# First attention of a two-layer audio tower: exponentials of two duos in one ScalarE instruction, its tail interleaved with the feed-forward start, GpSimd's blanks split up behind its chains of norms

## The reference, cut to what matters

```python
h = _L0_tok_ref(x, w, b)                        # keep 179 of 256 tokens, by score
h = h + _L0_attn_ref(_layernorm(h), ...)        # "first attention", additive:
    # score[h,t,s] = sum_d tanh(q[t,d] + k[s,d]) * ws[d] + bs;  softmax over s;  @ v;  @ Wo.T + bo
h = h + _L0_ffn_ref(_layernorm(h), ...)         # 192 -> 768, gelu, rounded to int8 steps, -> 192
h = h + _L1_attn_ref(_layernorm(h), ...)        # x rounded to int8 steps of max|x|/127 over ALL of x;
    # 12 heads of 16, base-2 softmax with a linear mantissa
h = h + _L1_ffn_ref(_layernorm(h), ...)         # 16 experts, each token through the one of largest gate
```

## Time and profile before

| | us |
|---|---|
| median of 3 runs (lowest, highest) | 1291.1 (1290.3, 1291.1) |
| profiled execution, its own time | 1291.22 |
| its span, first to last instruction | 1289.5 |
| first attention, first to last tanh | 64.5 to 803.2 |
| tail and feed-forward | 803.2 to about 905 |
| busy time: PE, DVE, ACT, POOL | 1088.6, 1071.3, 1006.7, 858.3 |

### The profile page before, as it was taken

The page is one execution under the profiler, slowest core; times in us unless marked ns, Lnnn a source line. Parts: engine busy times, 40 slices in busy tenths (PEclk is TensorE's granted clock), DMA queues, the critical chain, the costliest instruction groups (busy, mean ns, idle before and its releaser), DMA issues. The chain is left out here.

```text
span 1289.5 us, 44108 instructions
## 1 busy us (share of the span) xinstructions
PE 1088.6 (84%) x18872; PEld 823.3 (64%) x18875; DVE 1071.3 (83%) x2070; ACT 1006.7 (78%) x966; POOL 858.3 (67%) x931
## 2 busy tenths in 40 slices
PE   4866887888888788888779877899999999998796
PEld 3544665566566566566656655799566777776595
DVE  8988999999999999999999997577666777888342
ACT  3499999999999999999999999588445555544242
POOL 3099899898889889888888999775001233334354
PEclk9999999999999999999999999999999999999898
DMA  5799999930000000000000000110000200002451
GB/s 161 238 359 359 357 341 326 336 119 11 11 2 11 10 10 4 11 11 2 11 11 2 12 10 2 52 23 1 2 3 3 68 18 18 17 20 60 135 154 45
DMA packets 78547, 107.84 MB, mean 84 GB/s; under 512 B 6963, under 2 KB 76489, under 8 KB 78356
## 3 DMA queue, kind: packets, MB, share of 16 engines
q1 hardware_dynamic: 67894, 91.62, 21.8%
q0 software_dynamic: 5360, 8.02, 1.9%
q10 hardware_dynamic: 5104, 5.43, 1.5%
HBM read 18.32 MB, written 83.85 MB: 79 GB/s over the span
## 5 line engine op out<-in xcount | busy, mean ns | idle before, releaser
L1007 ACT ACTIVATE work<-work 128x2864 f32<-128x2864 f32 (+1 forms) x272 | 694.1, 2626 | 4.0 <-POOL work L446 3.0
L446 POOL TENSOR_TENSOR work<-shared 128x1253 f32<-128x1253 f32 (+1 forms) x272 | 612.9, 2268 | 87.7 <-PE psum L2050 77.7
L2050 PE MATMUL psum<-work,ws_place 128*32 128x179 f32 x8640 | 400.5, 323 | 139.4 <-ACT work L1007 131.1
L446 DVE TENSOR_TENSOR work<-psum,shared 128x1611 f32<-128x1611 f32 (+3 forms) x288 | 488.0, 1722 | 0.7 <-PE psum L2050 0.3
L2050 PEld LDWEIGHTS psum<-work,ws_place 128*32 128x32 f32 x8640 | 266.2, 111 | 239.7 <-ACT work L1007 181.0
L2250 PE MATMUL psum<-shared 32*32 32x179 f32 (+1 forms) x3456 | 99.1, 326 | 1.2 <-DVE peaks L1658 0.7
L1388 DVE SCALAR_TENSOR_TENSOR p_sb<-psum,bs_col,s_top 128x358 f32<-128x358 f32 x144 | 82.0, 570 | 14.9
L996 ACT ACTIVATE pt_region<-psum,bs_neg 128x384 f32<-128x384 f32 x144 | 89.0, 619 | 3.6 <-PE psum L2062 3.6
L902 POOL DMA_INDIRECT xs_dram<-w_store,slot_i x24 | 28.5, 1188 | 81.3 <-DVE slot_i L1758 75.2
L1385 DVE TENSOR_REDUCE s_top<-psum 128x2 f32<-128x358 f32 x144 | 71.7, 498 | 9.5 <-PE psum L2050 8.7
L2062 PE MATMUL psum<-ident,p_sb 128*128 128x128 f32 x416 | 78.6, 297 | 0.0
(11 more groups left out here) (444 smaller groups left out, 2010.6 us busy)
## 6 DMA issues: line engine op xcount, KB each, us to landing
xs_dram<-pad_row SPq DMA_DIRECT2D x23, 3088.0 KB, 28.5
pt_region<-xs_dram SPq DMA_DIRECT2D x19, 193.0 KB, 2.5
pt_region<-xs_dram ACTq DMA_DIRECT2D x19, 193.0 KB, 2.6
xs_dram<-pad_row SPq DMA_DIRECT2D x1, 2895.0 KB, 28.4
pt_region<-v_sb SPq DMA_DIRECT2D x22, 96.0 KB
work<-in_x SPq DMA_DIRECT2D x2, 768.0 KB, 9.8
work<-in_x ACTq DMA_DIRECT2D x2, 768.0 KB, 12.5
work<-in_L_ffn_W2T SPq DMA_DIRECT2D x1, 1536.0 KB
```

The source lines that it names most:

```text
L446: ins = eng.tensor_tensor(dst[:, a * KEEP:e * KEEP].rearrange("p (u s) -> p u s", s=KEEP), k[:, h * KP:h * KP + KEEP].unsqueeze(1).to_broa ...
L1007: act.activation(a, a, ACT.Tanh).then_inc(tanh_done, 1)
L2050: ins = pe.matmul(bank_s[p % 2][32 * quad:32 * quad + 32, at:at + KEEP], ws_place[:, j, :], arg_slot(n)[:, u * KEEP:(u + 1) * KEEP], start ...
```

## The change

Five edits:

1. `exps(b, n)` takes two duos (2n, 2n+1) in one ACT instruction of 768 columns, read out of both banks and written to both duos' places; the ninth duo stays alone. They stand after the tanh of groups 8, 12 and 16, and of groups 3 and 4 of the next batch. `turn_duo` waits accordingly, and the ninth duo always lies in the second bank. An ACT instruction of batch 15 that stood ahead of its last tanh (duo 4) now stands behind it.
2. In the tail PE does `ffn_turn(-1)` behind g of 3 instead of 2; `ffn_turn(0)` ahead of `ffn_hidden(0)` behind g of 5; `ffn_hidden(1)` behind g of 9; and `ffn_turn(1)` behind g of 11. Steps 0 and 1 of the feed-forward loop keep only `ffn_out`, and step 1 waits for the last residual add and its statistics.
3. ACT loads the gelu's table behind the first copy of a transposed input instead of ahead of it, and copies the second one ahead of batch 0's gelu.
4. DVE normalizes batch 2 at g of 2 of the tail and clips batch 0's hidden layer at g of 14, both out of the loop's first steps.
5. POOL's blanks behind the first one are cut into seven pieces, `later_blanks(j)`, and each stands behind `again_norms(j)`. The ones of v1 (`qv_blank` 3 and 4) are in the last piece, behind `again_norms(6)`. PE's wait for `qv_blank` 4 stays where it is.

```diff
+EXPS = -(-DUOS // 2)
...
+        pt_banks = psum[:, 2048:3072].rearrange("p (k c) -> p k c", c=512)
...
+        def pt_bank(k):
+            return bank_pt[1 if k == DUOS - 1 else k % 2]
         def duo(k):
...
             pool.memset(xn3[:, 1::2, :], 0.0).then_inc(qv_blank, 1)
-            pool.memset(ctx1[:, :, :], 0.0)
-            pool.wait_ge(wq_step, 6)
-            for n in (2, 3):
-                pool.memset(stage[n][:, 1, 0:D], 0.0)
-            pool.memset(ew2[:, 1, :], 0.0).then_inc(ew_blank, 1)
-            for n in range(2):
-                pool.memset(eh[n][:, :], 0.0)
-            for n in range(2):
-                pool.memset(q1[n][:, :, :], 0.0)
-                pool.memset(k1[n][:, :, :], 0.0)
-                ins = pool.memset(v1[n][:, :, :], 0.0)
-            ins.then_inc(qv_blank, 1)
-            pool.wait_ge(qv_blank, 2)
-            for n in range(2):
-                pool.memset(v1[n][:, :, HD:HD + 1], 1.0).then_inc(qv_blank, 1)
-                pool.memset(eh[n][:, D:D + 1], 1.0).then_inc(eh_blank, 1)
+            def later_blanks(n):
+                if n == 0:
+                    pool.memset(ctx1[:, :, :], 0.0)
+                    pool.wait_ge(wq_step, 6)
+                    for m in (2, 3):
+                        pool.memset(stage[m][:, 1, 0:D], 0.0)
+                if n in (1, 2):
+                    half = ew2[:, 1, EXPERTS * D // 2 * (n - 1):EXPERTS * D // 2 * n]
+                    ins = pool.memset(half, 0.0)
+                    if n == 2:
+                        ins.then_inc(ew_blank, 1)
+                if n == 3:
+                    for m in range(2):
+                        pool.memset(eh[m][:, :], 0.0)
+                if n in (4, 5):
+                    m = n - 4
+                    pool.memset(q1[m][:, :, :], 0.0)
+                    pool.memset(k1[m][:, :, :], 0.0)
+                    ins = pool.memset(v1[m][:, :, :], 0.0)
+                    if m == 1:
+                        ins.then_inc(qv_blank, 1)
+                if n == 6:
+                    pool.wait_ge(qv_blank, 2)
+                    for m in range(2):
+                        pool.memset(v1[m][:, :, HD:HD + 1], 1.0).then_inc(qv_blank, 1)
+                        pool.memset(eh[m][:, D:D + 1], 1.0).then_inc(eh_blank, 1)
...
                 again_norms(j)
+                later_blanks(j)
...
-            def exps(b, k):
-                p, w = b * DUOS + k, duo(k)
-                if k == 0:
+            def exps(b, n):
+                lo, hi = 2 * n, min(2 * n + 2, DUOS)
+                w = duo(hi - 1)
+                if n == 0:
                     need(act, ctx_psum, 2 * b - 2)
-                act.wait_ge(turned, p + 1)
-                act.activation(pt[b % 2][:, 0:w + 1, k, :],
-                               bank_pt[p % 2][:, 0:128 * (w + 1)].rearrange("p (s c) -> p s c", c=128),
-                               ACT.Exp, bias=bs_neg[:, :], scale=1.0).then_inc(exp_done, 1)
+                act.wait_ge(turned, b * DUOS + hi)
+                if hi - lo == 2:
+                    turned_keys = pt_banks[:, :, 0:384].rearrange("p k (s c) -> p k s c", c=128)
+                    act.activation(pt[b % 2][:, :, lo:hi, :].rearrange("p s k c -> p k s c"), turned_keys,
+                                   ACT.Exp, bias=bs_neg[:, :], scale=1.0).then_inc(exp_done, 1)
+                else:
+                    act.activation(pt[b % 2][:, 0:w + 1, lo, :],
+                                   pt_bank(lo)[:, 0:128 * (w + 1)].rearrange("p (s c) -> p s c", c=128),
+                                   ACT.Exp, bias=bs_neg[:, :], scale=1.0).then_inc(exp_done, 1)
...
                         act.activation(a, a, ACT.Tanh).then_inc(tanh_done, 1)
-                    if g % 2 and g >= 7 and real(b):
-                        exps(b, (g - 7) // 2)
-                    if g in (0, 1, 3, 4) and real(b - 1):
-                        exps(b - 1, DUOS - 4 + (0, 1, 3, 4).index(g))
-            act.preload_act_table(ACT.Gelu)
+                    if g in (8, 12, 16) and real(b):
+                        exps(b, (g - 8) // 4)
+                    if g in (3, 4) and real(b - 1):
+                        exps(b - 1, EXPS - 2 + g - 3)
...
-                if isinstance(i, int) and i == 0:
-                    ffn_gelu(i, par)
-                    ffn_turned(i, par)
-                else:
-                    ffn_turned(i, par)
-                    ffn_gelu(i, par)
+                ffn_turned(i, par)
+                ffn_gelu(i, par)
             ffn_turned(-1, 1)
+            act.preload_act_table(ACT.Gelu)
             staged(act, ffn_step, (1, 0))
...
+            def hidden_round(b):
+                dve.wait_ge(gelu_done, b + 1)
+                need(dve, y_psum, b - 1)
+                dve.tensor_scalar(hq[b % 2][:, :, 0:KEEP], gelu[b % 2].bitcast(I32).rearrange("p (c t) -> p c t", c=HT),
+                                  -128.0, 127.0, ALU.max, ALU.min).then_inc(hq_ready, 1)
             for b in range(B + 1):
...
                         ins.then_inc(hq_blank, 1)
+                        dve.wait_ge(f_xT_psum, 1)
+                        ffn_norm(2, 0)
+                    if b == B and g == 14:
+                        dve.wait_ge(hq_blank, 1)
+                        hidden_round(0)
             def ffn_step(i):
-                if real(i + 2):
+                if real(i + 2) and i > 0:
                     dve.wait_ge(f_xT_psum, i + 1)
                     ffn_norm(i + 2, i % 2)
                 if real(i - 2):
                     ffn_add(i - 2)
-                if real(i - 1):
+                if real(i - 1) and i > 1:
                     hidden_round(i - 1)
...
                 dve.scalar_tensor_tensor(r, y_int, s_out[:, :], r, ALU.mult, ALU.add).then_inc(f_added, 1)
-            def hidden_round(b):
-                dve.wait_ge(gelu_done, b + 1)
-                need(dve, y_psum, b - 1)
-                dve.tensor_scalar(hq[b % 2][:, :, 0:KEEP], gelu[b % 2].bitcast(I32).rearrange("p (c t) -> p c t", c=HT),
-                                  -128.0, 127.0, ALU.max, ALU.min).then_inc(hq_ready, 1)
...
                 p = b * DUOS + k
-                bank, src = bank_pt[p % 2], p_sb[p % 2]
+                bank, src = pt_bank(k), p_sb[p % 2]
                 pe.wait_ge(smax_done, p + 1)
-                need(pe, exp_done, p - 1)
+                need(pe, exp_done, EXPS * b + (k // 2 if k else -1))
                 for s in range(duo(k) + 1):
...
                     if g == 5:
-                        pe.wait_ge(exp_done, DUOS * b)
+                        pe.wait_ge(exp_done, EXPS * b)
                         pe.wait_ge(v_ready, b)
...
                         if b == B:
-                            pe.wait_ge(f_xT_ready, 1)
+                            pe.wait_ge(f_xT_ready, 2)
                         for t, bank in enumerate((bank_out, bank_pre)):
...
-                if not isinstance(i, int) or i > 0:
+                if not isinstance(i, int) or i > 1:
                     ffn_turn(i, par)
                     ffn_hidden(i, par)
+                if isinstance(i, int) and i == 1:
+                    pe.wait_ge(resid_added, 2 * B)
                 ffn_out(i, par)
...
                     after_scores(b, g)
-                    if b == B and g == 2:
+                    if b == B and g == 3:
                         pe.wait_ge(smax_done, B * DUOS)
                         pe.wait_ge(wq_step, 6)
                         ffn_turn(-1, 1)
                     if b == B and g == 5:
+                        ffn_turn(0, 0)
                         ffn_hidden(0, 0)
+                    if b == B and g == 9:
+                        ffn_hidden(1, 1)
                     if b == B and g == 11:
-                        ffn_turn(0, 0)
+                        ffn_turn(1, 1)
             pe.wait_ge(hq_blank, 1)
-            pe.wait_ge(exp_done, B * DUOS)
+            pe.wait_ge(exp_done, B * EXPS)
             staged(pe, ffn_step, (1, 1))
```

## The result

The changed kernel takes 1283.4 us in the median (1281.3 to 1284.3 in 5 runs), against 1291.1 for the kernel before in the same turns: a ratio of 0.9936 with a 95% interval of 0.9923 to 0.9950. It is faster, by 7.7 us. The forecast was 1280.6 us, range 1277.0 to 1286.5. The profiled execution took 1281.3 us (span 1279.6) and is the quickest of the five.

The account below looks back on a forecast made before the run. ACT was taken to bound the first attention, single waits the tail and behind the feed-forward. Profiled: 1291.2 - 9.1 (joint exponentials) - 4.5 (tail) + 3.1 (blanks) = 1280.7, so median 1280.6 us; range 1277 to 1286.5.

Parts of the forecast that it names:

- What bounds it: First attention: ACT bounds until DVE's reserve of 0.88 us a batch is used up; tail and behind feed-forward: single waits.
- Edit 1: First attention: joint exponential costs 0.80 instead of 0.94, saving 9.1 us together (bounds 11.6 and -0.8).
- Edits 2 to 4: Tail: batch 2's hidden layer begins 4.5 us earlier, 1.4 of it for a half clock that does not come.
- In the loop they cost nothing: Feed-forward loop: cut-up blanks cost nothing; the first chain starts earlier, but PE's period does not depend on it.
- Edit 5 at the end: Ahead of second attention: PE waits for the ones before its warm-ups; 1.8 plus 1.3 for half clock, +3.1 us.
- The sum: Whole kernel: profiled execution 1291.2 - 9.1 - 4.5 + 3.1 = 1280.7, so 1280.6 us for a median.
- case A: Whole kernel: all terms come as summed, 1280.6 us, own range 1278 to 1283; chance 0.60.
- B: End: no price there, clock holds or maximum comes later anyway; 1277.5 to 1279.3 us; chance 0.10.
- C: First attention: DVE becomes bound or early batches give nothing, half of 9.1 lost; 1285.2 us; chance 0.13.
- D: First attention: joint exponential saves nothing, 0.94 for 768 columns; 1289.7 us, no change by measure; chance 0.06.
- F: First attention: joint exponential costs more than two, slower; 1296.3 us at 1.05 a pair; chance 0.05.
- E: Tail: gives nothing because the last add, 2.5 later, delays as much as is taken out; 1285.1 us; chance 0.06.

Follow-up runs that it names:

- e8_half_tanh: Changed kernel with each tanh over only half its columns; a batch takes 44.66 us instead of 45.38, the loop 709.15 against 726.84.
- e4_no_blanks_edit: Changed kernel with the blanks back in one piece ahead of the first chain of norms; 1285.1 us.
- e6_ones_earlier: Changed kernel with the ones of v1 written behind the sixth chain instead of the seventh; 1278.7 us, ratio 0.9898.
- e1_joint_only: Kernel before with only the joint exponentials added; 1282.1 us against 1291.1.
- e2_tail_only: Kernel before with only the new order of PE, DVE and ACT in the tail; 1293.6 us.
- e3_blanks_only: Kernel before with only POOL's blanks cut up behind the chains of norms; 1295.9 us against 1291.1.
- e7_wait_chain: Kernel before, blanks untouched, with PE also waiting for the last chain of norms ahead of its warm-ups; 1295.6 us against 1291.6.
- e5_wait_behind: Changed kernel with PE's wait for the ones of v1 moved behind its 33 warm-up products; 1280.9 us, ratio 0.9904.

## Why the prediction was right, and where it was not

**What bounds it.** Right. ACT stays full in the loop after the change, and e8_half_tanh puts the next bound, DVE, 0.7 us below it in a steady batch.

**Edit 1.** Right in mechanism and size. The forecast was 9.1, from 0.14 a pair. The slot above shows 0.78 for a pair instead of 0.80; a steady batch, from its first tanh to the next one's, fell from 45.95 to 45.38, which is 0.57 or 0.14 for each of four pairs. The loop's -11.86 flatters it: the first tanh came 2.4 later in that execution, and it comes anywhere from 64.3 to 67.5 whatever the kernel (64.34 in e4_no_blanks_edit and 67.31 in e6_ones_earlier, both with edit 1). The last tanh's end is the better mark. It averages 803.2 over the four executions without edit 1 (803.17, 802.51, 804.07, 803.06) and 794.5 over the five with it and whole tanh (793.68, 794.25, 793.98, 796.42, 794.38): 8.7 us. The medians of e1_joint_only give 9.0. Batch 0 gave nothing (46.05 us, 46.01 before); the last batch, to its last tanh's start, gave 1.36, since work was also moved behind that tanh. The rule of 0.3 us per ACTIVATE that the prediction weighed (the Trainium skill, ScalarE: Activation LUTs, Rules for kernel authors) would have made 19; the start-to-start gap in the row was the better guide. DVE's wait for q, 0.47, is close to the 0.3 forecast, but it is not the whole reserve: the new wait of 0.3 for the output product belongs to it.

**Edits 2 to 4.** Right for the tail: 4.57 against 4.5, the half clock gone, 1.55 of idle time where I had some 1.3. The exact hit is partly luck. By itself the tail's edit gives 5.2 (19.61 in e2_tail_only); with edit 1 beside it the tail is 0.65 longer (20.26 in e4_no_blanks_edit), because, it seems, of the exponentials of batch 15 that edit 1 puts behind the last tanh, which the prediction took to be hidden. The 1.7 of it that the half clock was worth is no fixed part of the kernel before: e3_blanks_only has the same idle time and went without it (23.16), while e1_joint_only and e7_wait_chain had it (24.84 and 24.77). But what it was worth to the whole depended on edit 5, which the prediction did not see.

**Edit 5 in the loop.** The step that failed is "In the loop they cost nothing", with its reason "The first chain starts earlier, but PE's period does not depend on it". I looked for a price of the pieces and did not ask what the whole block cost if it stayed. The idle time of 2.81 that I read for POOL behind a chain belongs to the later ones; in the kernel before, the second chain starts 0.18 us behind the first, because POOL is late. The kernel before already had the sign of it, in POOL's and DVE's timelines:

```profile
828.81 2.66 POOL L785 MEMSET work<- 128x3072 f32 x1 [0.15 <-POOL rstd L731]
...
846.27 0.60 DVE L1254 BATCH_NORM_STATS2 stats<-resid 128x6 f32<-128x192 f32 x2
848.17 0.73 DVE L1542 TENSOR_SCALAR work<-resid,mean,rstd 128x192 f32<-128x192 f32 x2 [1.29 <-POOLq L878]
```

DVE waited 1.29 us for the first chain behind the blanks, short enough for PE not to notice. Edits 2 to 4 bring the feed-forward nearer to the last tanh and move POOL the other way: it waits for the statistics of the last residual add, which now comes later. Counted from the last tanh's end, POOL's blanks start at 28.6 in e4_no_blanks_edit instead of 25.6 (822.62 - 793.98, 828.81 - 803.17). DVE is ready for its first normalization at 40.13 instead of 43.71, 3.58 earlier, and gets the chain's result at 46.79 instead of 45.00, 1.79 later. 1.29 + 3.58 + 1.79 is the 6.66 of e4_no_blanks_edit. The error left the sum alone, since both edits were made together. It would have spoiled a forecast of either one: the medians of e1, e2 and e3 differ from before by -9.0, +2.5 and +4.8, which adds up to -1.7, and all three together give -7.7.

**Edit 5 at the end.** Right in mechanism, a bit too small: 3.81 against 3.1, still within the bounds of 1.8 and 4.2. The last chain kept its place as assumed: it ends 3.7 us behind the last product's start, before as after (905.67 - 901.93, 891.81 - 888.08). But from its end to the first warm-up it is 892.78 - 891.81 = 0.97, not 0.35: the memsets end at 892.19, 0.38 behind the chain, and PE starts 0.59 behind them, which the sum left out. So the idle time was 3.54 instead of 2.9, and that term is 4.70 + 7.1 - 9.42 = 2.4 instead of 1.8. The remaining 1.4 is the half clock, forecast at 1.3: it lasted 6.8 us, not 3.4, but only 3.3 of them fell on the warm-ups. Whether it falls there at all varies: in this execution it began before the idle time that edit 5 makes, in e3_blanks_only and e7_wait_chain 1 us into it (903.3 and 903.9). e5_wait_behind and e6_ones_earlier take it back; e7_wait_chain makes it without moving a blank. The rule weighed beside this term (the Trainium skill, TensorE: Matmul & The Clock Gate, HAM oscillation) pointed the right way: a half clock came in all four profiled executions in which PE idles ahead of the warm-ups (the kernel after, e3_blanks_only, e7_wait_chain and e8_half_tanh). In e6_ones_earlier one of 3.4 us came without that idle time, too.

**The sum.** The forecast change of the profiled execution was -10.5 and it was -9.9. This closeness is partly luck too, since the half clocks that fell or did not fall are in it. The median is another matter: -7.7, that is 2.8 above the forecast of 1280.6 and just outside the range of 1278 to 1283 that stood beside case A, though the mechanism is A's. One part is plain: the profiled execution happened to be the quickest of five (the other four 1283.0 to 1284.3). No run has a profile of one of those four, so where they lose their 2 us stays open. What can differ between executions of one kernel is seen in the profiled ones: the first tanh by 3 us, of which the loop takes part back, single stretches of half clock by 1.7 each, and the fourth batch of the loop, 45.4 in the profiled execution of the kernel after and 47.0, 47.9 and 48.5 in those of e1_joint_only, e4_no_blanks_edit and e5_wait_behind, with ACT waiting for DVE.

**The rivals.** B (no price at the end) is out: 13.23 against 9.42. C is out for this kernel by DVE's remaining 0.47 and 0.3, though near; its other half, that early batches give nothing, holds for batch 0 alone. D and F are out by 0.78 a pair. E, that the tail gives nothing, is out as stated, but in its result it is what e2_tail_only shows. The later add that it names has a part in it, by a way it did not name: POOL's blanks and first chain come behind that add's statistics.

## What to carry to other kernels

When a stage is brought nearer to the one ahead, list the engines whose own work does not move with it, or moves the other way. POOL's blanks (9 us without the first one, which stayed) were harmless until DVE came 3.6 us earlier and POOL 1.8 later, and DVE's 1.29 us wait showed how little room there was. Work cut up and moved behind later work takes its semaphore with it: look for whoever waits for the last piece, and move either the last piece one step up or the wait one step down (3.4 to 3.6 us of the stage here for one line; 2.5 and 4.8 in the medians). And compare stages from a mark that does not inherit the start's jitter; the loop's length alone would have credited edit 1 with 3 us too many.

## What was not expected of the hardware

- An exponential out of two PSUM banks in nested order shows no price for the second bank: 768 columns in 0.78 from start to start, 384 in 0.47, so 0.81 ns per further column and 0.16 fixed.
- Idle time alone does not decide the half clock. In PE's timeline of e3_blanks_only the tail has the 2.64 us of the earlier trace rows, but the products behind run at full clock from the first, 0.47 for two where they took 0.81:

```profile
823.09 0.63 PE L2022 MATMUL psum<-ident,norm_wide 128*128 128x128 f32 x4 [2.64 <-DVE norm_wide L1484]
823.56 0.47 PE L2015 MATMUL psum<-fx,w_store 128*128 128x179 f32 x2
```

  Likewise 2.20 us ahead of twelve products was followed by 3.4 us at half clock in e6_ones_earlier and 2.21 in e5_wait_behind by none, with the warm-ups starting at once in both. The kernel after idles 2.20, works 1.16, idles 3.54, and gets 6.8 us, which begin at the end of the 1.16, ahead of the 3.54. In e4_no_blanks_edit they begin 2.9 us into 4.38 of idle time.
- DVE's norm of two 192-column tiles takes 0.65 us by itself, and 3.32 beside POOL's 3072-column memset; the clamp of `hq` takes 0.72 and 2.48. That the memset is the cause is argued from the times side by side, not tested. DVE's and POOL's timelines of e2_tail_only:

```profile
830.75 3.32 DVE L1473 TENSOR_SCALAR norm_wide<-resid,mean,rstd 128x192 f32<-128x192 f32 x2
...
835.17 2.48 DVE L1482 TENSOR_SCALAR pt_region<-pt_region 128x1074 bf16<-128x1074 int32 x1
```

```profile
830.52 2.66 POOL L791 MEMSET work<- 128x3072 f32 x1 [0.15 <-POOL rstd L737]
...
834.42 2.65 POOL L796 MEMSET work<- 128x3072 f32 x1
```
